# A mixture-of-experts stage: counting by subtracted tiles, experts written out, rows found two experts at a time

## What is computed

```python
oh = jax.nn.one_hot(e, E, dtype=jnp.int32)
pos = jnp.take_along_axis(jnp.cumsum(oh, 0) - 1, e[:, None], 1)[:, 0]
valid = pos < CAP                       # CAP = 256
buf = jnp.zeros((E, CAP + 1, h), x.dtype).at[e, pos_c].set(x[token])[:, :CAP]
g = jnp.einsum('ech,ehi->eci', buf, w_gate)
u = jnp.einsum('ech,ehi->eci', buf, w_up)
y = jnp.einsum('eci,eih->ech', jax.nn.silu(g) * u, w_down)
out = jnp.zeros((n, h), jnp.float32).at[token].add(y_slots * w_slot[:, None])
```

## Time and profile before

| what | us |
|---|---|
| median of three runs | 3311.04 |
| the profiled execution | 3304.55 |
| its span, first to last instruction | 3302.7 |
| counting, first transfer issued to `total` ready | 2810.68 to 2839.09 |
| expert phase to the first gather | 2839.65 to 2851.13 |
| first to last scatter of an expert (64) | 2869.94 to 3290.60 |

### The profile page before, as it was taken

One profiled execution on the slowest core, in us unless ns is written; L12 is line 12 of the kernel. 1 busy time (PEld: TensorE's weight loads), 2 busy tenths in 40 slices (PEclk: granted clock), 3 DMA queues, 4 the chain that ended last, 5 costly groups with the idle time before them and its releaser, 6 DMA issues. The chain is left out here.

```text
span 3302.7 us, 55009 instructions
## 1 busy us (share of the span) xinstructions
PE 2943.3 (89%) x18817; PEld 2370.4 (72%) x18817; DVE 2808.4 (85%) x4597; ACT 2730.5 (83%) x5297; POOL 2259.9 (68%) x940
## 2 busy tenths in 40 slices
PE   6999999999999999999999999999999986665664
PEld 4777777777777777777777777777777775544543
DVE  4899999999999999999999999999999997344432
ACT  5999999999999999999999999999999995211110
POOL 1777777677777777676767777776767774377776
PEclk8999999999999999999999999999999998688887
DMA  3112222122222222121112222222222121477774
GB/s 111 58 59 68 70 70 70 58 64 64 70 70 70 70 70 70 61 70 64 62 59 69 70 70 70 70 70 70 70 70 70 51 65 30 118 145 152 148 150 75
DMA packets 196160, 252.80 MB, mean 77 GB/s; under 512 B 45664, under 2 KB 174144, under 8 KB 195904
## 3 DMA queue, kind: packets, MB, share of 16 engines
q1 hardware_dynamic: 171328, 211.73, 20.4%
q0 software_dynamic: 24576, 37.77, 6.9%
HBM read 188.36 MB, written 61.08 MB: 76 GB/s over the span
## 5 line engine op out<-in xcount | busy, mean ns | idle before, releaser
L345 POOL TENSOR_TENSOR hid<-hid,c_all 128x1536 f32<-128x1536 f32 x512 | 1768.4, 3460 | 842.2 <-DVEq L607 821.0
L612 DVE TENSOR_TENSOR_SCAN hid<-decay,hid,psB 128x1024 f32<-128x1024 f32 x512 | 1201.5, 2347 | 82.8 <-PE psB L914 35.2
L386 ACT ACTIVATE decay<-dt,a_neg 128x383 f32<-128x383 f32 x2048 | 1085.8, 604 | 0.5 <-issue 0.2
L914 PE MATMUL psB<-ident,dbu_t 128*128 128x128 f32 x6144 | 852.2, 275 | 87.9 <-DVE hid L612 61.8
L374 ACT ACTIVATE dbu_t<-dtu_t,b_t 128x512 f32<-128x512 f32 x1376 | 893.2, 710 | 4.1 <-PE psB L914 4.0
L914 PEld LDWEIGHTS psB<-ident,dbu_t 128*128 128x128 f32 x6144 | 700.0, 141 | 200.2 <-issue 87.1
L926 PE MATMUL psY<-ident,hid 128*128 128x128 f32 x6144 | 754.3, 273 | 0.1
L926 PEld LDWEIGHTS psY<-ident,hid 128*128 128x128 f32 x6144 | 687.2, 141 | 0.6 <-POOL hid L345 0.4
L612 DVE TENSOR_TENSOR_SCAN hid<-decay,psB 128x512 f32<-128x512 f32 x512 | 623.7, 1218 | 9.6 <-PE psB L914 5.2
L996 PE MATMUL psM<-u,w_dt 128*128 128x384 f32 x1024 | 351.5, 487 | 3.8 <-ACT u L416 3.1
L1407 ACT ACTIVATE e_side<-e_psL,e_in_tile 128x128 f32<-128x128 f32 x128 | 45.8, 363 | 261.9 <-DVE e_in_tile L1531 261.2
(11 more groups left out here) (148 smaller groups left out, 3260.6 us busy)
## 6 DMA issues: line engine op xcount, KB each, us to landing
c_all<-bc_rows_dram SPq DMA_DIRECT2D x128, 768.0 KB, 5.0
out_dram<-h SPq DMA_DIRECT2D x64, 384.0 KB, 5.7
h<-out_dram SPq DMA_DIRECT2D x32, 384.0 KB, 3.5
x_weights_dram<-normed SPq DMA_DIRECT2D x32, 384.0 KB, 2.6
xt<-in_x_t_dram SPq DMA_DIRECT2D x32, 375.0 KB
xs<-in_x_dram SPq DMA_DIRECT2D x32, 256.0 KB
e_wg<-in_gate_dram SPq DMA_DIRECT2D x64, 128.0 KB, 2.8
e_wu<-in_up_dram SPq DMA_DIRECT2D x64, 128.0 KB, 3.0
```

The lines of the kernel that those rows point to most:

```text
L345: nc.gpsimd.tensor_tensor(hid[k % 4][:, :, :], hid[k % 4][:, :, :], c_all[:, k, :].unsqueeze(1).to_broadcast([P, CH, L]), ALU.mult).then_i ...
L386: last = nc.scalar.activation(decay[k % 4][:, c, 1:L], dt[q][:, c, 1:L], ACT.Exp, scale=a_neg[:, c, k:k + 1])
L612: nc.vector.tensor_tensor_scan(h[:, lo:hi], flat(decay[k % 4])[:, lo:hi], flat(psB)[:, lo:hi], h[:, lo - 1:lo] if j else 0.0, ALU.mult, AL ...
L914: last = nc.tensor.transpose(flat(psB)[:, i * P:(i + 1) * P], dbu_t[k % 2][:, t, c * P:(c + 1) * P], ident[:, :])
```

## The change

In the counting block DVE subtracts neighbouring tiles of the table first (`steps`, one subtraction of 128 x 1552 16-bit numbers for each part of 16 experts), and PE makes one product per expert in place of two. At its end there are two small products in place of one (`n_prior` and `n_apart`), and ACT copies one result, DVE the other. Loops in this block are written out.

In the expert block all 64 experts are written out on all engines; register waits and `s_turn` are gone. `find_rows` handles 2 experts at a time (`PAIR`), 32 times in place of 8. Only 6 experts (`LOCATED`) are located ahead in place of 16. POOL's order is scatter e, gather e + 4. PE turns expert e + 1 in place of e + 2 ahead of `down` e, and `up` e + 1 stands behind `down` e. DVE stages experts e + 4 and e + 5 when it has scaled an even expert e.

```diff
+        step = [sb(f"n_step{q}", [P, NT + 1, NE // CG], BF16) for q in range(2)]
+        tri = sb("n_tri", [P, P + 1], BF16)
+        prior = sb("n_prior", [P, P], BF16)
+        apart_i = sb("n_apart_i", [P, P], I32)
+        apart = sb("n_apart", [P, P], BF16)
...
-            nc.gpsimd.memset(tri[:, 0, 0:P], 1.0).then_inc(s_t0, 1)
-            pool.wait_ge(s_t0, 1)
-
-            nc.gpsimd.affine_select(out=tri[:, 0, 0:P], in_=tri[:, 0, 0:P], compare_op=ALU.is_ge, fill=0.0,
+            nc.gpsimd.memset(tri[:, :], 1.0).then_inc(s_t0, 1)
+            nc.gpsimd.memset(prior[:, :], 1.0).then_inc(s_t0, 1)
+            pool.wait_ge(s_t0, 2)
+            nc.gpsimd.affine_select(out=tri[:, 0:P], in_=tri[:, 0:P], compare_op=ALU.is_ge, fill=0.0,
                                     base=0, pattern=[[1, P]], channel_multiplier=-1).then_inc(s_t1, 1)
+            nc.gpsimd.iota(apart_i[:, :], pattern=[[1, P]], base=0, channel_multiplier=-1).then_inc(s_ap, 1)
+            nc.gpsimd.affine_select(out=prior[:, :], in_=prior[:, :], compare_op=ALU.is_ge, fill=0.0,
+                                    base=-1, pattern=[[1, P]], channel_multiplier=-1).then_inc(s_t1, 1)
...
+                    pe.wait_ge(s_st, g + 1)
                 after(pe, s_uc[q], i)
                 for k in range(UB):
-                    g, e = divmod(j * UB + k, NE // CG)
-                    for d in range(2):
-                        last = nc.tensor.matmul(
-                            psU[q][0:R, k // 2, (k % 2) * (P + 1):(k % 2 + 1) * (P + 1)],
-                            chosen[:, g, 1 - d:1 - d + R, e], tri[:, d, :], start=(d == 0), stop=(d == 1))
+                    e = (j * UB + k) % (NE // CG)
+                    last = nc.tensor.matmul(psU[q][0:R, k // 2, (k % 2) * (P + 1):(k % 2 + 1) * (P + 1)],
+                                            step[g % 2][:, :, e], tri[:, :], start=True, stop=True)
...
-            nc.tensor.matmul(psT[0:R, 0:NE], tri[0:R, 0, 0:R], diff[0:R, :, P], start=True,
+            nc.tensor.matmul(psT[0][0:R, 0:NE], prior[0:R, 0:R], diff[0:R, :, P], start=True,
+                             stop=True).then_inc(s_tp, 1)
+            pe.wait_ge(s_t2, 1)
+            nc.tensor.matmul(psT[1][0:R, 0:NE], apart[0:R, 0:R], diff[0:R, :, P], start=True,
                              stop=True).then_inc(s_tp, 1)
...
+            act.wait_ge(s_tp, 2)
+            nc.scalar.activation(total[0:R, :], psT[1][0:R, 0:NE], ACT.Copy).then_inc(s_tot, 1)
...
+            def steps(g):
+
+                dve.wait_ge(s_ld[g], 16)
+                after(dve, s_u, (g - 1) * (NJ // CG))
+                nc.vector.tensor_tensor(step[g % 2][:, :, :], chosen[:, g, 1:NT + 2, :], chosen[:, g, 0:NT + 1, :],
+                                        ALU.subtract).then_inc(s_st, 1)
+
+            steps(0)
+            steps(1)
+            for i in range(NJ // 2):
                 dve.wait_ge(s_u, 2 * i + 2)
                 nc.vector.tensor_copy(diff_of(2 * i + 1), product(1)).then_inc(s_uc[1], 1)
-            dve.wait_ge(s_tp, 1)
-            nc.vector.tensor_copy(total[0:R, :], psT[0:R, 0:NE]).then_inc(s_tot, 1)
+                if i in (1, 3):
+                    steps(2 + i // 2)
+            dve.wait_ge(s_tp, 2)
...
-    STAGED = 6
-    NR = NE // EB
-    LOCATED = 2
+    LOCATED = 6
+    PAIR = 2
     FIN = 5
     R = NT + 1
     UW = P + 2
-    W = EB * NH
+    W = PAIR * NH
...
-            with sp.Fori(1, NE // EB) as i:
-                for q in range(EB):
-                    sp.wait_ge(s_yo, EB * i + q - EB + 1)
-                    sp.sem_inc(s_turn, 1)
-                    load(EB * i + q, q)
...
             for e in range(AHEAD):
-                gather(e, e)
+                gather(e)
             pool.wait_ge(s_zst, 16)
-
-            def expert(i, e, q):
-                if exists(e + AHEAD):
-                    gather(e + AHEAD, (q + AHEAD) % EB)
-                scatter(e, q)
-
-            each(pool, expert)
+            for e in range(NE):
+                scatter(e)
+                if e + AHEAD < NE:
+                    gather(e + AHEAD)
...
-            def expert(i, e, q):
-                if exists(e + 1):
-                    up(i + (q + 1) // EB, e + 1, (q + 1) % EB)
-                if exists(e + 2):
-                    turn(i + (q + 2) // EB, e + 2, (q + 2) % EB)
-                if exists(to_locate(e, q)[0]):
-                    gather_counts(*to_locate(e, q))
-                down(i, e, q)
...
+            for e in range(LOCATED):
+                gather_counts(e)
+            turn(0)
+            up(0)
+            for e in range(NE):
+                if e + 1 < NE:
+                    turn(e + 1)
+                if e + LOCATED < NE:
+                    gather_counts(e + LOCATED)
+                down(e)
+                if e + 1 < NE:
+                    up(e + 1)
 
         @block.vector
...
-                if q == 1 and (not isinstance(i, int) or 0 < i < NR - 1):
-                    find_rows(i + 1)
-                if exists(e + STAGED):
-                    after(dve, s_sc, 16 * NH * (e + STAGED - EB + 1))
-                    stage(e + STAGED, (q + STAGED) % EB)
-                if exists(to_locate(e, q)[0]):
-                    enter_tiles(*to_locate(e, q))
...
-            for e in range(LOCATED * EB):
-                if e + 1 < LOCATED * EB:
-                    pass_tiles(e + 1, (e + 1) % 2)
-                enter_tiles(e, e % 2)
-                if e % EB == EB - 1:
-                    find_rows(e // EB)
-                if e == EB - 1:
-                    for j in range(STAGED):
-                        stage(j, j)
-            copy_turned(0, 0)
-            copy_turned(1, 1)
-            each(dve, expert)
+            pass_tiles(0)
+            for e in range(LOCATED):
+                if e + 1 < LOCATED:
+                    pass_tiles(e + 1)
+                enter_tiles(e)
+                if e % PAIR == 1:
+                    find_rows(e // PAIR)
+                    for j in (e - 1, e):
+                        if j < AHEAD:
+                            stage(j)
+            copy_turned(0)
+            for e in range(NE):
+                activate(e)
+                if e + LOCATED < NE:
+                    pass_tiles(e + LOCATED)
+                if e + 1 < NE:
+                    copy_turned(e + 1)
+                scale(e)
+                if e % PAIR == 0 and e + AHEAD < NE:
+                    if e > 0:
+                        find_rows((e + AHEAD) // PAIR)
+                    for j in range(e + AHEAD, e + AHEAD + PAIR):
+                        stage(j)
+                if e + LOCATED < NE:
+                    enter_tiles(e + LOCATED)
 
 
 def audio_tower_kernel(nc, x, w, out):
```

155 lines of the change are left out of this document (66 added, 89 removed).

## The result

The changed kernel took 3286.47 us (median of five runs, 3278.35 to 3291.01), the kernel before beside it 3309.82 us. The ratio is 0.993, with a 95% interval from 0.9916 to 0.9943, so 23 us less (19 to 28). A second measurement of the same two kernels gave 0.9941 (0.9924 to 0.9958), 14 to 25 us less.

A forecast was written before the change was run, and what follows sets the result against it. Landing of dependent scatters was taken to bound the expert phase, PE the counting. Terms -5.1 - 7.8 - 2.5 + 5 = -10.4 us gave execution 3294.2, or 3300.6 for the median, range 3293.5 to 3310.

The forecast's parts named there:

- What bounds the kernel: Expert phase: each 6.59 us period is 1.6 + 0.3 + 1.6 of POOL issuing scatters and 3.0 of landing, gathers within it.
- PE and DVE have room: Expert phase: neither engine is the bound; of 90 us PE is busy 58 and DVE 39.
- about ten instruction transfers: Expert phase: a sign the forecast is right, transfers spread over the phase with the late scatters beside them.
- Part 1, counting: Counting block: its end comes 5.1 us earlier, 7.0 with a fast subtraction, as PE makes half the products.
- the round trip over one accumulator: Counting block: product batch, wait, DVE copy and return take 1.94 us, above PE's 1.46, so this becomes the bound.
- The subtraction: Counting block: the new DVE operation on 1552 columns takes 1.77 us; 0.6 by another row, 0.96 by the skill page.
- insertion cost: Counting block: the third and fourth subtractions, queued ahead of a DVE copy, hold PE back about 0.53 us each, together 1.1.
- the fast end of my range for this part: Counting block: -7.0 us in place of -5.1, if the subtraction is quick.
- Part 2, the head: From counting to first scatter: 7.8 us earlier, with the first gather 4.9 earlier; up to 2.5 lost if gathers land later.
- Part 3, the periods: 63 periods between first and last scatter: 6.59 us stays; +5 for instruction transfers and -2.5 for the start, together +2.5.
- the mean of 0.8 us: Expert phase: lateness per instruction transfer, from five earlier ones; about 6 more transfers then cost +5 us, between 0 and 10.
- The -2.5 for the burst: First periods: half of the 4.5 us lost ahead of scatter 11 is regained as weight loads spread out, between -4 and 0.

The follow-up runs named there:

- half_gather: Changed kernel without the second gather (rows 128 to 255) of experts from the ninth on; ratio to the kernel before 0.9978, median period 6.68 us.
- two_tables: Changed kernel with odd experts' rows added into a spare table, so a scatter waits only for the one two experts before; ratio to the kernel before 0.9895.
- three_acc: Changed kernel with three accumulators for the counting products in place of two; 3283.91 us, ratio to the kernel before 0.994, counting 18.0 us.
- pe_order: Changed kernel with PE's order put back to up e + 1, turn e + 2, counts, down e; ratio to the kernel before 0.9973.
- located16: Changed kernel with 16 experts located ahead of the loop in place of 6; ratio to the kernel before 0.998, first scatter at 37.5 us.
- experts_only: Kernel before with the changed expert function alone, counting as before; ratio to the kernel before 0.9972.
- again_before: The kernel before, unchanged, profiled and measured again; ratio to the kernel before 1.0008, first scatter at 33.6 us.
- warm: three_acc with 13 unread products in PE's idle time between the first experts' counts and turn 0; ratio to the kernel before 0.9938.
- warm_short: warm with only the 7 extra products behind the counts of experts 4 and 5; ratio to the kernel before 0.9929.

## Why the prediction was too small

**What bounds the kernel: right.** half_gather and two_tables show the period as landing, with POOL's issue 0.14 us behind it. Also right was that PE and DVE have room, and the forecast of about ten instruction transfers.

**Part 1, counting: -5.1 forecast, -8.2 measured.** The mechanism was right, the round trip over one accumulator, which three_acc confirms. Three sizes were off, all in the same direction. The subtraction is 0.96 us and not 1.77: products start 0.9 us later in the block than before, not 1.9. The nearest row had two sources as well, but 32-bit numbers, and I took it over the 16-bit row with one source; the truth lay between them. An estimate from the Trainium skill, VectorE: DVE Perf Modes, "The perf-mode tier table", was 0.96 us, and the trace agrees to the last digit. Since 0.96 fits between two copies, no insertion cost, where 1.1 was charged. And the round trip is 1.78 us, not 1.94: a copy starts 1.03 us behind the start of its batch and not 1.10, and PE goes on 0.06 us behind the copy and not 0.14. Seven times 0.16 is 1.1. Together 3.1 us. Even the fast end of my range for this part, -7.0, kept the slow round trip.

**Part 2, the head: -7.8 forecast, -8.2 in the first pair of traces, -9.3 in the mean.** The new head is what was worked out: from `total` to the first scatter 23.0 forecast, 22.6 measured, and 22.1 to 23.3 in all traces of that head. Within it two small misses cancel: the first gather came 0.7 us sooner than forecast, and `turn` 0 followed it by 6.1 us and not 5.7. pe_order confirms the part of the order (2.2 us), located16 the part of the smaller number located. What was off is the old head: the trace before had one of its quick passes, 30.3 us where the four traces have 29.7 to 33.6 and a mean of 31.4. With `up` 1 ahead of `down` 0 it is exposed to the time at which the clock rises, and its first copy waits for DVE, which has 16 experts to locate. In the new head that copy waits for `turn` 0 alone.

**Part 3, the periods: +2.5 forecast, nothing measured.** The count of instruction transfers was right, the price was wrong: +5 became about +1.7. The step that failed is the mean of 0.8 us, drawn from five delays in a stretch where the weight loads of the start came together too; I had put the largest delay down to its transfer alone, 1.9 us at scatter 1; in the eleven traces in which no such transfer falls there, this scatter is late by 0.4 to 1.4 us all the same. The -2.5 for the burst can't be told from the spread. The first 11 periods of the trace I read were late by 4.6 us, the most of the four old ones; the old ones have 3.1 in the mean and the nine new ones 2.2. Over all periods the mean over nine traces of the new phase is 419.2, over four of the old 419.5. That the loop and `s_turn` were free was right.

**The rest.** The terms as measured sum to -8.2 - 9.3 - 0.3 = -17.8 us. The second measurement has that within its interval (14 to 25), the first doesn't quite (19 to 28). Of the 14.1 us between forecast and median, 3.1 are the counting, 1.5 the head and 2.8 the periods. Another 1.2 are the kernel before, whose median beside the changed one was 3309.82 and not the 3311.04 that I had started from. The other 5.5 I can't assign. The sequence part varies by 12 us between traces with the same code, so one trace can't say whether it plays a part. Terms of one sum that were each bounded with care left a range that was too narrow above all on the side of the gain: each doubt had been settled against it.

## What to carry over

When work moves from one engine to another, price it by a row that is alike in number type and in count of sources. When engines hand few accumulators round, as here, work that fits into a gap of that round costs nothing. Price the head of a phase from several traces if it runs while the clock is low, and put work that the first result doesn't need behind it. Where a phase waits for landings of dependent scatters, shorter work elsewhere changes nothing: here taking the dependence away was worth 15 to 16 us in the first 60 periods of the traces, and one gather less for each expert was worth nothing.

## What the runs showed of the hardware

- A subtraction of two 16-bit tensors of 1552 columns takes 0.96 us on DVE, 0.62 ns a column with all fixed cost in it. With two 32-bit sources it is 354 ns for 192 columns, 1.8 ns a column counted the same way (1.0 ns for each column beyond 96).
- PE's clock stood at 0.50 throughout the old counting block, with PE busy 23.45 of 25 us in 128 products without a gap (the stretch of the kernel before is below); in the head it rose 2.8 to 3.8 us behind the start of `up` 0 in 13 of the 16 traces, and 5.0, 5.5 and 9.2 us behind it in located16, experts_only and again_before. It fell back 2.9 us behind the last product, in a wait of 3.4 us (warm), and 2.5 us behind it, just after a wait of 2.1 us (warm_short).

```profile
2813.00:2838.00 25.00, 23.45 (x128) 23.29 (x128) 5.21 (x8) 4.83 (x8) 0.00 (x0) 0.50 0.14 49
```

- A transfer of 16 KB of instructions holds one DMA engine for 0.9 to 1.9 us and costs the waiting scatter 0.4 us in the mean; PE's instructions come over the queue q8, SP's over q14 (by the two paddings).
- With 40 semaphore counts an expert in its queue PE stands idle for 3.4 us an expert in the mean and the kernel takes 2% more than the changed one, while for 30 on SP, which has time, no cost is seen.
